# Batch-major copies of the mixer's B and C tiles on ScalarE, and factor loads in four transfers

## The chip, the cores and the metric

The kernel runs on one core of a Trainium2 chip. The metric is the device time of the whole program in microseconds (us). TensorE appears in the profile as PE (matrix products) and PEld (loads of its stationary operand), VectorE as DVE, ScalarE as ACT, GpSimd as POOL and SyncE, which issues nearly all DMAs here, as SP.

## The reference

The program is one decoder layer in fp32 for 4 sequences of 1024 tokens, 256 wide: a recurrent mixer, cross-attention and a mixture of experts. Only the mixer is touched. Cut to what matters, it computes for 32 heads with 32 states of 16 channels each:

```python
bc = einsum('bti,oi->bto', value, W_bc).reshape(B, T, 32, 4, 32)
bc = bc / (sqrt(sum(bc * bc, -1, keepdims=True)) + 1e-8)
Bz, Bx, Cz, Cx = bc[..., 0, :], bc[..., 1, :], bc[..., 2, :], bc[..., 3, :]
def step(z, s):                       # one token
    S = 1 / (1 + dt * k + dt * dt * A)
    z = S * (z - dt * A * s + dt * Bz * u)
    s = s + dt * z + dt * Bx * u
    y = sum_n(Cz * z) + sum_n(Cx * s)
```

## The kernel before

The mixer works through 16 units `u` of 64 time steps of all four batches, 256 columns, stored with time outside and batch inside: column `4t + b`. Each unit has four group pairs `gp`, of two head groups each; a head group is four heads, and a head has 32 partitions (a lane group). Within a unit the recurrence is turned into matrices: VectorE steps a 2x2 transition `phi` through 64 steps (`evolve`, L917 and L923), scales the four projections B and C by norms and by decay factors, and multiplies them with `phi` (`inputs` L956 to L970 for B, `read_out` L978 to L993 for C). The results are written back into `bc`.

TensorE then reads `bc` one batch at a time, so with a step of four numbers (16 bytes): it transposes the B tiles (`inputs_turned`, L629, `bc` as stationary operand), forms the causal products B times C (`causal_products`, L642, both operands from `bc`) and applies C to the carried state (`mixed_states`, L662, `bc` as moving operand), followed by L672 and L682. Between these stand the projections of the group pair that comes three places later (L604, 32 matmul records for each half) and the sums of squares for its norms (L618). Once in a unit there are the output products of the unit before (L691).

ScalarE evacuates projections (L757, L760), computes norms with three table loads (L767 to L771), scales the step coefficients of the next unit (`coefs`, L738, after their DMA) and copies transposes (L779). VectorE multiplies the norms by further factors (`factors`, L943); SyncE stores them to DRAM (L495) and loads them back, broadcast to the 32 partitions of each lane group, as `fb` and `fc` (L502).

Every engine works through its own list in the order in which the code writes it, and semaphores tie the lists together. So a wait on one instruction holds back all that is written behind it on that engine. The order of VectorE in a unit is, in short: `read_out` 0, `post` 3 of the unit before, `factors`, `ends`, `inputs` 1, `read_out` 1, `residual`, `inputs` 2, `mask` 0, `read_out` 2, `factors`, `post` 0, `inputs` 3, `mask` 1, `read_out` 3, then `evolve` of the next unit in pieces with `post` and `mask` between them, and `inputs` 0 of the next unit. `post` (L1013 to L1023) folds TensorE's result into output and state and uses `m1` and `m2`, the scratch tiles that `inputs` and `read_out` use too.

Of the kernel before, what the change touches and what calls it, by code (L numbers as in the profile page):

```python
# [13 lines left out]
P = 128  # L14
# [12 lines left out]
LANES = G * CH  # L27
EPS_LN, EPS_BC = 1e-5, 1e-8
# [14 lines left out]
def constants():  # L43
# [4 lines left out]
    hn = np.arange(G)[None] * J + jn[:, None]  # L48
    c["sel"] = (hn[:, :, None] == np.arange(H)[None, None]).astype(np.float32)
    c["causal"] = (np.arange(L)[None] >= (np.arange(P) % L)[:, None]).astype(np.float32)  # L50
    r = np.ones((P, UT), np.float32)
# [284 lines left out]
def mixer(nc, d, st, wbc, x, x1):  # L336

    with ExitStack() as ctx:
# [10 lines left out]
        sel = sb("sel", [P, G, H])  # L349
        causal = sb("causal", [P, L])  # L350
        resetm = sb("resetm", [P, UT])
# [10 lines left out]
        uu = sb("uu", [P, 2, 2, LANES])  # L362
        pinv = sb("pinv", [P, G, UT])
        iqe = sb("iqe", [P, LANES])
        pend = sb("pend", [P, 2, LANES])
# [11 lines left out]
        m1 = sb("m1", [P, 2, UT])  # L377
        m2 = sb("m2", [P, 2, UT])
# [45 lines left out]
        out_ready = sem("out_ready")  # L424
        bt_full = sem("bt_full")
# [13 lines left out]

        xv = x.rearrange("(q r u s) m -> u r s q m", q=2, r=2, s=L)  # L440
# [148 lines left out]
        def _(pe):  # L589
# [18 lines left out]
            def summed(u, gp, i):  # L608
# [7 lines left out]
                for v in range(2):  # L616
                    c = first + v
                    mm = pe.matmul(ssp[H * c:H * c + H, 0:UT], sel[:, g, :], sq[:, v, :],  # L618
                                   start=(i < 2), stop=(i >= 2))
                mm.then_inc(sums_done, 1)  # L620

            def inputs_turned(u, gp):
                n = GP * u + gp
                pe.wait_ge(in_ready, n + 1)
                if n > 0:
                    pe.wait_ge(km_ready, n)
                for v in range(2):
                    for b in range(B):
                        mm = pe.transpose(kp[:, v, b * P:(b + 1) * P],  # L629
                                          turns(bc[:, gp, v].rearrange("p i t -> p (i t)"))[:, :, b], ident[:])  # L630
# [17 lines left out]
            def mixed_states(u, gp, more, un, gn):  # L648
# [8 lines left out]
                for b in range(B):  # L657
                    for i in range(2):
                        for v in range(2):
                            for j in range(J):  # L660
                                r = slice(N * j, N * j + N)
                                pe.matmul(yp[r, b * L:(b + 1) * L], hpad[r, v, i, b, :],  # L662
                                          turns(bc[r, gp, 2 + v, i, :])[:, :, b],
# [60 lines left out]
        def _(act):  # L724
# [55 lines left out]

            def states(u, gp):
# [18 lines left out]
            for u in range(NU):  # L800
                for gp in range(GP):
                    un, gn = (u, GP - 1) if gp == 0 else (u + 1, gp - 1)
                    more = un < NU
                    inputs_turned(u, gp)
                    if more:
                        projected(un, gn, 0)
                        projected(un, gn, 1)
                    states(u, gp)
# [5 lines left out]
                    if more:  # L814
                        projected(un, gn, 2)
                        projected(un, gn, 3)
                        norms(un, gn)
                    if gp == 0 and u + 1 < NU:
                        coefs(u + 1)

        @block.vector
        def _(dve):
# [107 lines left out]
            def accumulate(u):  # L930
                for h in range(2):
                    dve.wait_ge(ln_ready, G * u + B * h + B)
                    v = pinv[:, B * h:B * h + B, :].rearrange("p g (t b) -> p (g t) b", b=B)
# [11 lines left out]
            def ends(u):  # L945
                dve.wait_ge(pinv_ready, u + 1)
                dve.wait_ge(iqe_in, 64 * (u + 1))
                link(V.tensor_copy(pend[:, 1, :].rearrange("p (g b) -> p g b", b=B), pinv[:, :, UT - B:UT]))
# [3 lines left out]
            def inputs(u, gp):  # L952
                n = GP * u + gp
                dve.wait_ge(fb_in, 128 * (n + 1))
# [1156 lines left out]
```

## Time and profile before

| | us |
|---|---|
| median of 3 runs | 3303.73 |
| lowest, highest | 3301.38, 3319.04 |
| profiled execution, whole time | 3292.49 |
| its span, first to last instruction | 3290.7 |
| busy in the span: PE, PEld, DVE, ACT, POOL | 2919.8, 2169.8, 2064.4, 1304.7, 286.7 |
| mean granted TensorE clock | 0.937 |

Busy time is the time in which an engine had an instruction at work. The mixer's units fill about 400 to 2090 us of the span; projections come before, cross-attention and experts behind. These rows of the page, in 40 slices of 82 us, show the mixer in slices 5 to 25:

```profile
PE   5885799999999999999999999589888399999996
DVE  5444898889889998999899888465562000111110
ACT  3443445454545554545454544133241021333332
PEclk9887899999999999999999999689899599999998
```

### The profile page before, as it was taken

Reading aid. Unit: us, or ns where it says so; the run is one execution under the profiler, and the core shown is the slowest. Engines: PE = TensorE matmul, PEld = TensorE weight load, DVE = VectorE, ACT = ScalarE, POOL = GpSimd, SP = SyncE. Lnnn points to the kernel's source line nnn. Section 1 sums busy time; section 2 is a strip of 40 time slices with the busy share of each in tenths; the row PEclk is TensorE's granted clock in tenths of the full one; section 3 lists DMA queues with packets and bytes.
Section 4 is the critical chain, followed back from the end, with each engine's and each line's share of the span. In section 5 each row is a group of like instructions: output and inputs, shape, how many; then the busy total and the mean of one; then the engine's idle time right before and its main releaser. Section 6 shows DMA issues by size and latency. Waiting matters only on the chain. (4 is left out here: it accounts for less than half of the span.)

```text
span 3290.7 us, 83944 instructions
## 1 busy us (share of the span) xinstructions
PE 2919.8 (89%) x34208; PEld 2169.8 (66%) x34208; DVE 2064.4 (63%) x7109; ACT 1304.7 (40%) x2250; POOL 286.7 (9%) x227
## 2 busy tenths in 40 slices
PE   5885799999999999999999999589888399999996
PEld 2343577777777877787788777433345166888885
DVE  5444898889889998999899888465562000111110
ACT  3443445454545554545454544133241021333332
POOL 0000000000000000000000000000004700443433
PEclk9887899999999999999999999689899599999998
DMA  6556333542444334433543352200053201778877
GB/s 235 151 151 177 91 85 77 121 104 76 95 117 104 81 95 118 108 83 88 124 104 87 82 128 69 79 1 1 1 203 113 98 28 36 208 201 204 207 200 216
DMA packets 333343, 373.98 MB, mean 114 GB/s; under 512 B 62395, under 2 KB 294988, under 8 KB 328268
## 3 DMA queue, kind: packets, MB, share of 16 engines
q1 hardware_dynamic: 310540, 340.22, 37.6%
q0 software_dynamic: 22464, 28.95, 4.3%
q8 instruction: 249, 4.08, 0.6%
q14 instruction: 90, 0.74, 0.1%
HBM read 269.18 MB, written 104.04 MB: 113 GB/s over the span
## 5 line engine op out<-in xcount | busy, mean ns | idle before, releaser
L604 PE MATMUL ring<-valt,wbc 128*128 128x256 f32 x4096 | 946.2, 387 | 29.0 <-DMA valt<-valt_scratch 26.9
L604 PEld LDWEIGHTS ring<-valt,wbc 128*128 128x128 f32 x4096 | 775.0, 193 | 169.4 <-issue 62.9
L757 ACT COPY bc<-ring 128x512 f32<-128x512 f32 x256 | 149.3, 583 | 739.1 <-PE ring L604 739.1
L917 DVE TENSOR_TENSOR uu<-phi,coef 128x64 f32<-128x64 f32 x2048 | 361.6, 218 | 2.1
L923 DVE TENSOR_TENSOR phi<-phi,uu 128x64 f32<-128x64 f32 x2048 | 361.3, 217 | 0.0
L2039 DVE TENSOR_SCALAR f_yr<-fp_y,f_meta 128x256 f32<-128x256 f32 x124 | 54.3, 480 | 413.3 <-PE fp_y L1856 413.3
L662 PE MATMUL yp<-bc,hpad 32*32 32x64 f32 x8192 | 260.2, 289 | 2.5 <-DVE hc L1023 2.5
L662 PEld LDWEIGHTS yp<-bc,hpad 32*32 32x32 f32 x8192 | 225.3, 121 | 53.3 <-issue 53.0
L1923 ACT ACTIVATE f_hT<-fp_h,f_b 128x256 f32<-128x256 f32 x248 | 117.4, 473 | 327.5 <-PE fp_h L1847 327.5
L1856 PE MATMUL fp_y<-f_w,f_hT 128*128 128x256 f32 x992 | 230.7, 386 | 7.9
L1723 POOL DMA_INDIRECT acc_scratch<-f_yr,f_meta x124 | 192.5, 1553 | 446.7 <-DVE f_yr L2039 300.1
L1847 PE MATMUL fp_h<-f_xrt,f_w 128*128 128x256 f32 x992 | 226.0, 381 | 0.8 <-ACT f_xrt L1912 0.8
L1710 POOL COPY f_xn<-f_gk 128x32 f32<-128x32 f32 x3 | 0.7, 242 | 2506.3 <-DVE f_rowid L2020 2502.9
L1856 PEld LDWEIGHTS fp_y<-f_w,f_hT 128*128 128x128 f32 x992 | 183.4, 190 | 45.0 <-ACT f_hT L1923 21.9
L1847 PEld LDWEIGHTS fp_h<-f_xrt,f_w 128*128 128x128 f32 x992 | 189.6, 191 | 27.3 <-issue 1.2
L618 PE MATMUL ssp<-sq,sel 128*32 128x256 f32 x1024 | 162.0, 394 | 41.0 <-ACT sq L760 40.7
L1972 DVE TENSOR_TENSOR xres<-fp_y,xres 128x1024 f32<-128x1024 f32 x10 | 12.2, 1225 | 268.9 <-PE fp_y L1778 134.8
L956 DVE TENSOR_TENSOR bc<-bc,fb 128x512 f32<-128x512 f32 x128 | 82.7, 687 | 129.0 <-DMA fb<-fac_scratch 128.4
L642 PEld LDWEIGHTS kp<-bc 32*64 32x64 f32 x8192 | 141.3, 203 | 32.2 <-issue 32.2
L1764 PE MATMUL fp_y<-f_ws,f_hT 128*128 128x256 f32 x512 | 124.6, 395 | 42.7 <-issue 42.7
L642 PE MATMUL kp<-bc 32*64 32x64 f32 x8192 | 153.0, 306 | 6.1 <-issue 3.7
L760 ACT ACTIVATE sq<-ring 128x512 f32<-128x512 f32 x256 | 153.1, 598 | 5.4 <-PE ssp L618 5.4
(227 smaller groups left out, 4070.9 us busy)
## 6 DMA issues: line engine op xcount, KB each, us to landing
f_w<-in_W_dram SPq DMA_DIRECT2D x128, 512.0 KB
coef<-par_scratch SPq DMA_DIRECT2D x128, 256.0 KB, 5.9
fb<-fac_scratch SPq DMA_DIRECT2D x512, 64.0 KB, 2.2
fc<-fac_scratch SPq DMA_DIRECT2D x512, 64.0 KB, 2.8
xg_scratch<-f_fill SPq DMA_DIRECT2D x16, 1032.0 KB, 17.3
f_xr<-xg_scratch SPq DMA_DIRECT2D x64, 258.0 KB
vtok_scratch<-p_vtok SPq DMA_DIRECT2D x32, 512.0 KB, 7.0
dub<-vtok_scratch SPq DMA_DIRECT2D x16, 1024.0 KB, 5.4
```

Source lines behind the costliest of these rows:

```text
L604: mm = pe.matmul(ring[:, p % 2, v * UT:(v + 1) * UT], wbc[:, k, g, first + v, :], valt[:, u % 2, k, :], start=(k == 0), stop=(k == 3))
L618: mm = pe.matmul(ssp[H * c:H * c + H, 0:UT], sel[:, g, :], sq[:, v, :], start=(i < 2), stop=(i >= 2))
L642: mm = pe.matmul(kp[L * i:L * i + L, j, b * L:(b + 1) * L], turns(bc[r, gp, v, i, :])[:, :, b], turns(bc[r, gp, 2 + v, i, :])[:, :, b], st ...
L662: pe.matmul(yp[r, b * L:(b + 1) * L], hpad[r, v, i, b, :], turns(bc[r, gp, 2 + v, i, :])[:, :, b], start=(b == 0 and i == 0 and v == 0), s ...
L757: nc.scalar.copy(bc[:, gp, first:first + 2, i // 2, :], o).then_inc(bc_ready, 1)
L760: nc.scalar.activation(sq[:], o, ACT.Square).then_inc(sq_ready, 1)
L917: made[k] = mark(V.tensor_tensor(uu[:, k].rearrange("p i (g b) -> p i g b", b=B), phi[:, t, ::-1, k, :].rearrange("p i (g b) -> p i g b", ...
L923: ins = V.tensor_tensor(phi[:, t + 1, :, k, :], phi[:, t, :, k, :], uu[:, k], ALU.add)
L1723: pool.indirect_dma_start(acc, bass.IndirectOffsetOnAxis(ap=meta[:, par, a, 0:1].bitcast(I32), axis=0), yr[:, par, a, :], None, compute_op ...
L1764: mm = pe.matmul(yp[:, 2 * (nb % 2) + a // 2, (a % 2) * DM:(a % 2 + 1) * DM], hT[:, e, f, a * P:(a + 1) * P], ws2[:, e, f, :], start=(e == ...
L1847: mm = pe.matmul(hp[:, f, 0:RT], w1[:, par, k, f * P:(f + 1) * P], xrt[:, par, k, :], start=(k == 0), stop=(k == 1))
L1856: mm = pe.matmul(yp[:, par, a * DM:(a + 1) * DM], hT[:, par, f, a * P:(a + 1) * P], w2[:, par, f, :], start=(f == 0), stop=(f == 3))
```

## The change

Four things change, all in the mixer.

1. `inputs` and `read_out` no longer write into `bc`. They write into new tiles `min_` and `mout`, in the same time-major order, and ScalarE copies these into `bc` in batch-major order (`turn_in`, `turn_out`: two copies of 128x512 each, four numbers of step on the reading side). TensorE's three readers of `bc` wait for the copies and read contiguous columns.
2. `min_` takes the place of `m1` and `m2` and also holds `uu` (scratch of `evolve`) and `pend` (scratch of `ends`). So `inputs`, `post`, `ends` and `evolve` on VectorE get waits on `turned_in`, and `read_out` one on `turned_out`.
3. Head rows in the factor and coefficient arrays in DRAM are ordered by lane group, then head group. A factor load is four DMAs of 128 KB in place of eight of 64 KB, and the coefficient and ratio loads read rows of 8 KB in place of 1 KB, with the same number of DMAs.
4. The call of `factors` behind `read_out` 2 moves inside it. `resetm` is halved, so the scans of `accumulate` are 16 of 128 elements in place of 8 of 256. `sel` is a sliding window of one narrow tile.

```diff
+        uu = min_[:, 1, 1, 0:4 * LANES].rearrange("p (k i l) -> p k i l", k=2, i=2)
+        pend = min_[:, 1, 1, 4 * LANES:6 * LANES].rearrange("p (i l) -> p i l", i=2)
...
-                return v.rearrange("(g j) t -> j g t", j=J)[j].unsqueeze(0).broadcast_to([N, G, v.shape[-1]])
+                return v.rearrange("(j g) t -> j g t", j=J)[j].unsqueeze(0).broadcast_to([N, G, v.shape[-1]])
...
-                src = st["fac"][n].rearrange("(c g i j) t -> g j i c t", c=4, g=GP, i=2)[gp]
+                src = st["fac"][n].rearrange("(c j g i) t -> g j c (i t)", c=4, j=J, g=GP)[gp]
                 for j in range(J):
-                    for c in range(2):
-                        sp.dma_start(dst[N * j:N * j + N, :, c, :],
-                                     src[j, :, c0 + c].unsqueeze(0).broadcast_to([N, 2, UT])).then_inc(signal, 16)
+                    sp.dma_start(dst[N * j:N * j + N].rearrange("p c i t -> p c (i t)"),
+                                 src[j, c0:c0 + 2].unsqueeze(0).broadcast_to([N, 2, 2 * UT])).then_inc(signal, 16)
...
             def inputs_turned(u, gp):
...
-                pe.wait_ge(in_ready, n + 1)
+                pe.wait_ge(turned_in, n + 1)
...
             def causal_products(u, gp):
...
-                pe.wait_ge(out_ready, n + 1)
+                pe.wait_ge(turned_out, n + 1)
...
-                                               turns(bc[r, gp, v, i, :])[:, :, b],
-                                               turns(bc[r, gp, 2 + v, i, :])[:, :, b],
+                                               by_batch(gp, v)[r, b * P + i * L:b * P + (i + 1) * L],
+                                               by_batch(gp, 2 + v)[r, b * P + i * L:b * P + (i + 1) * L],
...
+            def turn_batches(m, c, gp, done):
+                for v in range(2):
+                    ins = nc.scalar.copy(by_batch(gp, c + v).rearrange("p (b i t) -> p i b t", b=B, i=2),
+                                         m[:, v].rearrange("p i (t b) -> p i b t", b=B))
+                ins.then_inc(done, 1)
...
             def evolve(u, t0, t1):
...
                     if u > 0:
                         dve.wait_ge(out_ready, GP * u)
+                        dve.wait_ge(turned_in, GP * u)
...
             def accumulate(u):
-                for h in range(2):
+                for h in range(4):
...
             def inputs(u, gp):
...
-                    V.tensor_tensor(bc[:, gp, 0, i, :], fb[:, i, 1, :], m[:, 1, :], ALU.subtract)
-                    ins = V.tensor_tensor(bc[:, gp, 1, i, :], m[:, 0, :], fb[:, i, 0, :], ALU.subtract)
+                    V.tensor_tensor(min_[:, 0, i, :], fb[:, 1, i, :], min_[:, 0, i, :], ALU.subtract)
+                    ins = V.tensor_tensor(min_[:, 1, i, :], min_[:, 1, i, :], fb[:, 0, i, :], ALU.subtract)
                 ins.then_inc(in_ready, 1)
...
             def read_out(u, gp, between=None):
...
+                if between is not None:
+                    factors(between)
+                if n > 0:
+                    dve.wait_ge(turned_out, n)
...
             def post(u, gp, read):
...
-                dve.wait_ge(out_ready, read)
+                dve.wait_ge(turned_in, read)
```

On ScalarE, in the middle of a unit (from the last norm activation of group pair 0 on), the list reads before:

```order
L771 ACTIVATE nr<-nr 128x256
L738 ACTIVATE coef<-coef,nega 128x256 x8
L779 COPY btt<-kp 128x512 x2
L757 COPY bc<-ring 128x2x256
L760 ACTIVATE sq<-ring 128x512
L757 COPY bc<-ring 128x2x256
L760 ACTIVATE sq<-ring 128x512
L788 COPY hpad<-hc 128x2x4x16 x2
```

and now, with `mout` and `min` as the names of the new tiles:

```order
L776 ACTIVATE nr<-nr 128x256
L788 COPY bc<-mout 128x2x4x64 x2
L743 ACTIVATE coef<-coef,nega 128x256 x8
L784 COPY btt<-kp 128x512 x2
L762 COPY bc<-ring 128x2x256
L765 ACTIVATE sq<-ring 128x512
L788 COPY bc<-min 128x2x4x64 x2
L762 COPY bc<-ring 128x2x256
L765 ACTIVATE sq<-ring 128x512
L807 COPY hpad<-hc 128x2x4x16 x2
```

Two copies of the C tiles of group pair 1 stand ahead of the coefficients, and two of the B tiles of group pair 2 between the two evacuations behind them. A unit has eight such pairs: three stand ahead of these rows (the first, `turn_in` of group pair 0, is ahead of everything else of the unit), two behind them (the second of these, `turn_in` of group pair 3, is behind the next norms), and one in group pair 2.

On VectorE, at the end of `read_out` 2 and `post` 0, the list with its waits now reads as follows; before, L943 (now L981) stood behind the last row of `read_out`, and none of these rows waited for a copy.

```order
L1028 TENSOR_TENSOR fc<-phi,bc 128x2x256 [waits dve_step] x2
L981 TENSOR_TENSOR nr<-nr,pq 128x256 [waits nr_ready]
L1033 TENSOR_TENSOR mout<-phi,bc 128x2x256 [waits turned_out]
L1033 TENSOR_TENSOR mout<-phi,bc 128x2x256
L1037 TENSOR_TENSOR mout<-fc,mout 128x2x256 [waits dve_step] x2
L1057 SCALAR_TENSOR_TENSOR min<-valt,skip,yp 128x256 [waits sg_in,turned_in,y_full]
```

The factor multiply moved ahead of four instructions, and `post` 0 (L1057) now waits for `turned_in`, which is the pair of `min` copies shown in ScalarE's list.

On SyncE's queue, the DMAs from the loads of group pair 2 up to the coefficients were before:

```order
L502 DMA fb<-fac_scratch 32x2x256 x8
L482 DMA sg<-sg_scratch 128x1024
L502 DMA fc<-fac_scratch 32x2x256 x8
L470 DMA pq<-par_scratch 32x256 x3
L472 DMA iqe<-par_scratch 32x8x4 x4
L462 DMA coef<-par_scratch 32x8x256 x4
```

and are now:

```order
L507 DMA fb<-fac_scratch 32x2x512 x4
L488 DMA sg<-sg_scratch 128x1024
L507 DMA fc<-fac_scratch 32x2x512 x4
L476 DMA pq<-par_scratch 32x256 x3
L478 DMA iqe<-par_scratch 32x8x4 x4
L468 DMA coef<-par_scratch 32x2048 x4
```

Eight DMAs fewer are issued ahead of the coefficients, whose rows are now whole.

## Rows read from the trace of the kernel before

**Rows 1.** the mixer's stretch: busy us (instructions) of PE, PEld, DVE, ACT, POOL, PEclk

```profile
400.00:2090.00 1690.00, 1618.58 (x27937) 1311.88 (x27936) 1527.76 (x5744) 823.00 (x1358) 0.00 (x0) 0.98 0.39 96
```

**Rows 2.** timeline, the residual sum: start us, us, engine, line, names, shapes

```profile
492.45 0.68 DVE L1030 TENSOR_TENSOR xs<-yp,xs 128x512 f32<-128x512 f32 x1
...
2030.37 0.68 DVE L1030 TENSOR_TENSOR xs<-yp,xs 128x512 f32<-128x512 f32 x1
```

**Rows 3.** waits in 400 to 2090 us: us in total, times, longest us

```profile
DVE bc L956 <- DMA fb<-fac_scratch: 123.6, 30, 8.4
```

**Rows 4.** timeline, VectorE, one unit: in brackets idle us before and releaser

```profile
1245.02 0.41 DVE L970 TENSOR_TENSOR bc<-m,fb 128x256 f32<-128x256 f32 x1
...
1268.00 1.29 DVE L956 TENSOR_TENSOR bc<-bc,fb 128x512 f32<-128x512 f32 x2 [1.23 <-DMA fb<-fac_scratch]
...
1290.54 1.29 DVE L956 TENSOR_TENSOR bc<-bc,fb 128x512 f32<-128x512 f32 x2 [7.70 <-DMA fb<-fac_scratch]
...
1302.84 0.36 DVE L917 TENSOR_TENSOR uu<-phi,coef 128x64 f32<-128x64 f32 x2
...
1330.95 4.77 DVE L935 TENSOR_TENSOR_SCAN pinv<-resetm,pinv 128x256 f32<-128x256 f32 x8
...
1347.17 1.23 DVE L1001 TENSOR_TENSOR km<-kp,causal 128x1024 f32<-128x1024 f32 x1
...
1355.10 0.42 DVE L970 TENSOR_TENSOR bc<-m,fb 128x256 f32<-128x256 f32 x1
```

**Rows 5.** timeline, ScalarE, the same unit

```profile
1275.25 0.42 ACT L771 ACTIVATE nr<-nr 128x256 f32<-128x256 f32 x1
1284.31 3.30 ACT L738 ACTIVATE coef<-coef,nega 128x256 f32<-128x256 f32 x8 [8.65 <-DMA coef<-par_scratch]
...
1288.93 0.59 ACT L760 ACTIVATE sq<-ring 128x512 f32<-128x512 f32 x1
...
1307.21 0.42 ACT L771 ACTIVATE nr<-nr 128x256 f32<-128x256 f32 x1
```

**Rows 6.** timeline, TensorE, the same unit and an earlier one at half clock

```profile
1245.49 1.23 PE L629 MATMUL kp<-ident,bc 128*128 128x128 f32 x8
...
1258.99 2.38 PE L642 MATMUL kp<-bc 32*64 32x64 f32 x128
1261.29 3.72 PE L604 MATMUL ring<-valt,wbc 128*128 128x256 f32 x16
...
1289.58 1.07 PE L618 MATMUL ssp<-sq,sel 128*32 128x256 f32 x4 [5.38 <-ACT sq L760]
1290.58 2.39 PE L642 MATMUL kp<-bc 32*64 32x64 f32 x128
...
518.57 5.51 PE L604 MATMUL ring<-valt,wbc 128*128 128x256 f32 x16
```

**Rows 7.** timeline, the issuing queue of SyncE: start us, us of issuing, count

```profile
1266.81 4.25 SPq L502 DMA_DIRECT2D fc<-fac_scratch  x8
...
1275.57 2.08 SPq L462 DMA_DIRECT2D coef<-par_scratch  x4
```

**Rows 8.** DMA issues: count, KB each, median us from issue to landing

```profile
coef<-par_scratch SPq DMA_DIRECT2D x128, 256.0 KB, 5.9
dub<-vtok_scratch SPq DMA_DIRECT2D x16, 1024.0 KB, 5.4
```

**Rows 9.** groups by shape in 0 to 300 us: busy us, mean ns

```profile
L257 ACT COPY p_vraw<-pp_ring 128x512 f32<-128x512 f32 x32 | 18.7, 585 | 60.3 <-PE pp_ring L211 60.3
L253 ACT COPY p_xnt<-pp_ring 128x512 f32<-128x512 f32 x16 | 15.7, 1082 | 6.1 <-PE pp_ring L205 6.0
```

**Rows 10.** weight loads of 64 columns: duration ns min/median/max

```profile
L216 PEld LDWEIGHTS pp_ring<-p_xnt,p_win x32: 132/136/137, 42.3 to 237.7; 128*64 128x64 f32 x32
...
L691 PEld LDWEIGHTS yp<-wout,sg x512: 192/193/226, 480.5 to 2094.5; 128*64 128x64 f32 x171
```

**Rows 11.** window about a rest of TensorE, columns as in Rows 1

```profile
1286.80:1293.70 6.90, 4.12 (x134) 3.10 (x135) 3.16 (x6) 4.19 (x11) 0.00 (x0) 0.51 0.43 134
```

More of the change, by code:

```diff
@@ L27 @@
 LANES = G * CH
+SW = H + G - 1
 EPS_LN, EPS_BC = 1e-5, 1e-8
@@ L424, in mixer @@
         out_ready = sem("out_ready")
+        turned_in = sem("turned_in")
+        turned_out = sem("turned_out")
         bt_full = sem("bt_full")
@@ L779, in inputs_turned, with turn_in, turn_out @@
                     nc.scalar.copy(btt[:, v], kp[:, v, :].rearrange("p (b m) -> p b m", b=B)).then_inc(btt_ready, 1)
+            def turn_batches(m, c, gp, done):
[3 more added lines that the diff above has]
+                ins.then_inc(done, 1)
+            def turn_in(u, gp):
+                act.wait_ge(in_ready, GP * u + gp + 1)
+                turn_batches(min_, 0, gp, turned_in)
+            def turn_out(u, gp):
+                act.wait_ge(out_ready, GP * u + gp + 1)
+                turn_batches(mout, 2, gp, turned_out)
             def states(u, gp):
@@ L803, in _ @@
                     more = un < NU
+                    if gp == 0:
+                        turn_in(u, 0)
                     inputs_turned(u, gp)
@@ L806, in _ @@
                         projected(un, gn, 0)
+                    if gp == 1:
+                        turn_in(u, 2)
+                    if more:
                         projected(un, gn, 1)
+                    if gp == 0:
+                        turn_out(u, 0)
+                    if gp == 2:
+                        turn_out(u, 3)
                     states(u, gp)
@@ L815, in _ @@
                         projected(un, gn, 2)
+                    if gp == 0:
+                        turn_in(u, 1)
+                    if gp == 1:
+                        turn_out(u, 2)
+                    if more:
                         projected(un, gn, 3)
                         norms(un, gn)
-                    if gp == 0 and u + 1 < NU:
-                        coefs(u + 1)
+                    if gp == 0:
+                        turn_out(u, 1)
+                        if u + 1 < NU:
+                            coefs(u + 1)
+                    if gp == 1:
+                        turn_in(u, 3)
         @block.vector
@@ L947, in ends @@
                 dve.wait_ge(iqe_in, 64 * (u + 1))
+                dve.wait_ge(turned_in, GP * u + 1)
                 link(V.tensor_copy(pend[:, 1, :].rearrange("p (g b) -> p g b", b=B), pinv[:, :, UT - B:UT]))
@@ L963, in inputs, with read_out @@
                     need(scaled[i])
[L964 to L967 removed]
+                    V.tensor_tensor(split(fb[:, :, i]), rows(1, 0, 2 * gp + i), twice(bc[:, gp, 0, i, :]), ALU.mult)
+                if n > 0:
+                    dve.wait_ge(turned_in, n)
+                other = [mark(V.tensor_tensor(split(min_[:, ::-1, i]), rows(0, 1, 2 * gp + i), twice(bc[:, gp, 1, i, :]),
+                                              ALU.mult)) for i in range(2)]
+                for i in range(2):
                     need(other[i])
[L969 to L970 removed]
+                    V.tensor_tensor(min_[:, 0, i, :], fb[:, 1, i, :], min_[:, 0, i, :], ALU.subtract)
+                    ins = V.tensor_tensor(min_[:, 1, i, :], min_[:, 1, i, :], fb[:, 0, i, :], ALU.subtract)
                 ins.then_inc(in_ready, 1)
[L973 removed]
+            def read_out(u, gp, between=None):
                 n = GP * u + gp
[L975 removed]
+                dve.wait_ge(fc_in, 64 * (n + 1))
                 if gp == 0:
                     dve.wait_ge(pinv_ready, u + 1)
[L978 removed]
+                decayed = [mark(V.tensor_tensor(fc[:, :, i], fc[:, :, i],
                                                 pinv[:, 2 * gp + i, :].unsqueeze(1).broadcast_to([P, 2, UT]), ALU.mult))
@@ L1053, in _ @@
                 mask(u, 0)
-                read_out(u, 2)
-                factors(n0 + 3)
+                read_out(u, 2, n0 + 3)
                 post(u, 0, n0 + 3)
@@ L2072, in layouts @@
     r["A_states"] = np.asarray(inputs["L0_attn_A_log"]).reshape(G, J * N).T
-    r["dt_bias_b"] = np.tile(np.asarray(inputs["L0_attn_dt_bias"]), B)[:, None]
+    r["dt_bias_b"] = np.tile(np.asarray(inputs["L0_attn_dt_bias"])[rows], B)[:, None]
     r["ctxT"] = np.asarray(inputs["ctx_768"]).transpose(0, 2, 1)
```

61 lines of the change are left out of this document (27 added, 34 removed).

## The prediction

> **What bounds the kernel now.** I read the windows view of the mixer first. In its 1690 us TensorE is busy 1618.6, VectorE 1527.8 and ScalarE 823.0 [rows 1]. Two engines are over 90% busy, so busy shares don't say which one sets the time. The page's chain that ended last covers only the experts and is no help here; the period of a unit is. The residual sum comes once a unit, and from 492.45 to 2030.37 there are 14 periods of 109.85 us [rows 2].
>
> The timeline of one unit tells who sets that period. I count from the end of VectorE's `inputs` 0, 1245.43 (1245.02 plus 0.41) [rows 4]. VectorE works without a hole except for 1.23 us ahead of `inputs` 2 and 7.70 us ahead of `inputs` 3, both for the factor DMA [rows 4]; in the whole stretch that wait is 123.6 us in 30 places [rows 3]. It starts `evolve` at 1302.84, 57.4 us in, and ends the next `inputs` 0 at 1355.52, 52.6 us later (I take 52.6, start to start) [rows 4]. TensorE starts its transposes 0.06 us after `inputs` 0 [rows 6] and rests once, 5.38 us, for a square of ScalarE [rows 6], which in turn had stood 8.65 us in front of `coefs` for its DMA [rows 5]. So VectorE's own list sets the period: about 101 us of work and 8.9 us of waiting for factors. TensorE follows closely but isn't waited for.
>
> **What the change removes.** TensorE: the causal products take 2.30 us for 128 records (1258.99 to 1261.29) at full clock, and 2.32 us at half clock (1290.58 plus 2.39, less overlap) [rows 6, 11]. An array that is not sped up by its clock is limited by the reading of its operands. A 64-column weight load takes 136 ns from contiguous columns and 193 ns with a step of 16 bytes [rows 10]. By that ratio the products lose 0.7 us, by a halved rate 1.15; I take 1.0 each, with 0 and 1.15 as ends. `mixed_states` should gain more, but most of it stands behind the last sum of squares of a group pair, and nobody waits for it: it counts as nothing.
>
> DMA: a factor load of eight takes 4.25 us to issue [rows 7], so four take 2.1. The load `fc` 2 stands ahead of the coefficients on the queue, which are issued at 1275.57 and land for ScalarE at 1284.31, 8.7 us later [rows 5, 7]. Four issues fewer are 2.1 us; and `fc` 2, which started behind the issue of `fb` 2, can start at once when `read_out` 1 is done, 0.7 us earlier. So the coefficients start at about 1272.8. A megabyte in 8 KB rows (`dub`) lands in 5.4 us, while one quarter of that in 1 KB rows takes 5.9 [rows 8]. So the coefficients land at about 1278.2, 32.8 us into the unit. The factor load of group pair 3 is stored 2.4 us earlier by the moved multiply and is shorter: both DMA waits of VectorE go, 8.9 us.
>
> **What it adds.** Eight pairs of copies on ScalarE per unit, 128x512 each. The trace has no ACT instruction that reads SBUF with a step of 16 bytes. A copy that steps on its writing side takes 1082 ns, a contiguous one 585 [rows 9]. These are the ends: 1.2 or 2.1 us for a pair. I take 2.1, since TensorE's weight loads show that the stepped read itself is slower [rows 10].
>
> The Trainium skill has a rule for either end. In "SBUF — State Buffer", section "Door 1: The DMA port swizzle", it says that SBUF has 16-byte cachelines and an access that goes to a new line each time pays; by it a pair takes the long time. TensorE's stepped loads agree with it [rows 10]. In "ScalarE: Activation LUTs", section "Rules for kernel authors", a budget of about 0.3 us plus 0.83 ns per element knows no step; by it a pair takes 1.45 us, near the short case. The 1082 ns of a stepped write contradict this second rule [rows 9]; no row here shows the read.
>
> What these copies delay is the point. `post` 0 and `evolve` now wait for `turned_in`, and ScalarE's list is in lockstep with TensorE's. The new path from `inputs` 0 to `evolve`:
> - `turn_in` 0: 2.1.
> - TensorE's transposes to the end of the norms, 1245.49 to 1275.67: 30.2, less 1.0: 29.2 [rows 5, 6].
> - `turn_out` 1: 2.1. It ends 33.4 in, behind the landing of the coefficients, so that wait is gone.
> - `coefs`, transposes copied, first evacuation: 1284.31 to 1289.52, 5.2 [rows 5].
> - TensorE's sums (1289.58) to the end of the next norms (1307.63): 18.05, less 1.0 for the products and 0.8 for work that was done here at half clock (an estimate: half of the 1.07 of the sums, and the start of the projection behind): 16.2 [rows 5, 6].
> - `turn_in` 3: 2.1.
>
> That is 56.9 us (54.2 with short copies). `evolve` follows, and VectorE's remaining 52.6 us, plus 0.4 for scans: eight take 4.77 us [rows 4], so 16 half as long take somewhat more for their fixed part (0 to 1). The period is 109.9 us (107.2), against 109.85. The 8.9 us of DMA wait have become waits for ScalarE at `post` 0 and at `evolve`. The multiply that moved gains nothing more, because `post` 0 waits anyway. SyncE's shorter list is waited for by nobody else.
>
> **The clock.** TensorE now runs out of work. At the end of a unit it has finished everything but the values when VectorE makes the last mask, and then waits for `evolve`'s rest, `inputs` 0 (mask done at 1348.40, `inputs` 0 at 1355.52: 7.1 us [rows 4]) and `turn_in` 0: a rest of 7 to 9 us in each unit where it had none. The trace shows what follows a rest: after 5.38 us of it the granted clock is 0.51 in the window 1286.80 to 1293.70, with the work back at 1289.58 [rows 6, 11], so 4.1 us are worked at the 1.2 GHz level and 2.1 us lost; in another unit a 16-record projection took 5.51 us in place of 3.72 [rows 6]. Now that lost time stands at the head of the path. I take 2.1 per unit; ends 0 and 3.4 (the whole window at half clock). Before, such rests were rare, with a mean clock of 0.98, and lay in VectorE's shadow [rows 1].
>
> **Sum.** Period 109.9 + 2.1 = 112.0, 2.15 more than before; 15 repeats give +32. The prologue waits for its first coefficients too; half of such a wait saved is -4 (estimate from the 8.65). The last unit's chain gets one more pair of copies, +2. Total +30. The profiled execution's own time is 3292.5 (span 3290.7), so it would be 3322; the median of the runs is 11.2 us above that execution, and on its footing the forecast is 3334 us.
>
> **Rivals.**
> 1. Short copies and the clock loss: 109.3 a unit, -8 in all, with the ends -2: 3294. For it: the copy that took 1082 ns steps on its writing side, and reading may be another matter [rows 9].
> 2. Long copies, no clock loss (TensorE's rest is broken up by small work): +1 -2, 3303.
> 3. The other side: ScalarE copies at the contiguous 585 ns and the clock holds. Then VectorE is the bound again except for some 6 us at `post` 0 and `evolve`; 107.2 a unit, -40 -2: 3262. It decides below about 0.9 us a copy when the clock holds, or below 0.5 us when it doesn't. Against it: the slow stepped loads and the half clock after a rest [rows 10, 11].
> 4. The change doesn't do what it says: contiguous columns don't speed the products, because it is the many small instructions that limit them. Then 2.0 more per unit: 3364. Against it: the stepped loads again, 193 ns for 136 [rows 10]. Of like size: coefficients that still take 8.7 us from their issue would land at 36.1, 2.7 later than ScalarE needs them, +40: 3374; a landing between the two is likelier.
>
> **Chances.** Forecast 0.46; rival 1 0.21; rival 2 0.15; rival 3 0.12; rival 4 0.06. A measurement here tells a change of 0.5%, 16.5 us, from none: faster is below 3287, slower above 3320. Rival 3 and a third of rival 1 are faster: with some spread 0.22. Rival 2 and the rest of rival 1, and a tenth of the forecast for a smaller clock loss, are the same: 0.29. Slower 0.49. The range takes rival 3 at its lower end and rival 4 at its upper: 3264 to 3360. The forecast's own range is 3315 to 3354 (clock loss 0.8 to 3.4).
>
> **What the profile after would show.** Right: no DMA wait on VectorE's L956 successor; idle there ahead of `post` 0 (some 5 us or more) and ahead of `evolve`; copies of 1.08 us; causal products near 1.3 us; TensorE busy at least 64 us less in the mixer (64 products, 1.0 each), with a rest of over 7 us at each unit's end and a clock near 0.93 there against 0.98 [rows 1]; coefficients landed before ScalarE asks. Wrong: copies near 0.6 us; a wait ahead of `inputs` 3 that is still the factor DMA's; a mixer clock unchanged; VectorE's period near 101.

## The result, and the profile after

The changed kernel takes 3410.18 us (median of 4 runs, 3408.04 to 3413.32) where the kernel before, on the same chip, takes 3311.39 (4 runs, 3301.38 to 3324.01). The ratio is 1.0311, with a 95% interval from 1.026 to 1.0362. So it is slower, as forecast, but by 99 us and not by 30, and the time lies above the range.

These rows of the windows view cover 14 units of the mixer each, from the second residual sum to the sixteenth; first the kernel before. The columns are those of [rows 1].

```profile
492.45:2030.37 1537.92, 1484.76 (x25069) 1202.17 (x25068) 1404.78 (x5322) 764.90 (x1259) 0.00 (x0) 0.98 0.40 98
```

The kernel after:

```profile
497.09:2146.60 1649.51, 1406.39 (x25092) 1117.16 (x25091) 1413.32 (x5434) 996.52 (x1484) 0.00 (x0) 0.92 0.37 91
```

A unit takes 1649.51 / 14 = 117.8 us where it took 109.85 [rows 2] and 112.0 were forecast. TensorE is busy 5.6 us less in each unit (1484.76 less 1406.39, over 14), ScalarE 16.5 more, and the clock fell from 0.98 to 0.92. What the engines wait for is seen in the waits view of the kernel after, 400 to 2090 us, first VectorE, then TensorE (us in total, times, longest us):

```profile
DVE min L1057 <- issue: 88.8, 15, 8.2
DVE min L955 <- ACT bc L788: 73.0, 15, 7.1
DVE min L1006 <- ACT bc L788: 41.6, 14, 3.5
DVE mout L1033 <- ACT bc L788: 26.6, 18, 1.7
DVE bc L995 <- DMA fb<-fac_scratch: 4.1, 7, 1.3
```

```profile
PE kp L634 <- ACT bc L788: 113.4, 14, 8.6
PE yp L677 <- issue: 39.9, 22, 4.0
PE yp L687 <- issue: 30.1, 13, 4.1
PE yp L687 <- DVE km L1045: 28.8, 18, 4.0
PE kp L647 <- issue: 13.7, 4, 3.7
PE kp L634 <- issue: 4.1, 3, 2.6
```

VectorE's wait for factor rows has gone from 123.6 [rows 3] to 4.1. In its place it stands 230 us for ScalarE's copies (L788); the row that names "issue" ahead of `post` (L1057) is the wait for `turned_in` too: in the unit below it starts at 1351.53, and the copies of `turn_in` 2 end at 1351.44. TensorE stands 8 us a unit for the first copy, and loses 88 us to "issue": it waits for nothing but its own instructions. In the same stretch of the kernel before, those "issue" rows come to 22.5 us. The row `L687 <- DVE km` is another thing: there TensorE really waits for VectorE's mask (`mask`, L1045), and goes on 0.04 us behind it.

The timeline of one unit shows where each piece lies. ScalarE (in brackets the idle us before, and the releaser):

```profile
1340.21 0.42 ACT L776 ACTIVATE nr<-nr 128x256 f32<-128x256 f32 x1
1340.53 2.10 ACT L788 COPY bc<-mout 128x512 f32<-128x512 f32 x2
1342.53 3.30 ACT L743 ACTIVATE coef<-coef,nega 128x256 f32<-128x256 f32 x8
1345.74 1.04 ACT L784 COPY btt<-kp 128x512 f32<-128x512 f32 x2
1348.34 0.58 ACT L762 COPY bc<-ring 128x512 f32<-128x512 f32 x1 [1.55 <-PE ring L609]
...
1367.72 0.42 ACT L776 ACTIVATE nr<-nr 128x256 f32<-128x256 f32 x1
1368.04 2.11 ACT L788 COPY bc<-min 128x512 f32<-128x512 f32 x2
```

TensorE in the same unit:

```profile
1308.55 1.97 PE L634 MATMUL kp<-ident,bc 128*128 128x128 f32 x8 [8.63 <-ACT bc L788]
...
1341.78 0.85 PE L687 MATMUL yp<-km,dub 128*32 128x64 f32 x19 [3.35 <-issue]
1342.56 1.97 PE L634 MATMUL kp<-ident,bc 128*128 128x128 f32 x8
1344.32 7.43 PE L609 MATMUL ring<-valt,wbc 128*128 128x256 f32 x32
1351.68 0.63 PE L623 MATMUL ssp<-sq,sel 128*32 128x256 f32 x4
...
1375.06 1.59 PE L647 MATMUL kp<-bc 32*64 32x64 f32 x128
```

VectorE:

```profile
1351.53 0.48 DVE L1057 SCALAR_TENSOR_TENSOR min<-valt,skip,yp 128x256 f32<-128x256 f32 x1 [6.36 <-issue]
...
1370.29 0.36 DVE L955 TENSOR_TENSOR min<-phi,coef 128x64 f32<-128x64 f32 x2 [4.13 <-ACT bc L788]
```

The hole (a gap in TensorE's work) of 3.35 us ahead of 1341.78 belongs to TensorE's supply of instructions. The DMA view of the kernel after, from 1334.0 to 1339.3 us, has only the data queue in it, at 93% of 16 engines:

```profile
q1 hardware_dynamic: 427, 1.15, 93.4%
```

and from 1339.3 to 1341.9, while TensorE stands, one packet of the queue that brings instructions, with the data queue nearly idle:

```profile
q1 hardware_dynamic: 37, 0.03, 3.1%
q8 instruction: 1, 0.02, 2.5%
```

That packet holds 16 KB, starts at 1339.33 and takes 1.04 us; TensorE goes on 1.4 us after its end. One such packet comes for each 256 instructions of TensorE, products and weight loads. This row is the kernel before's 14 units, in which TensorE ran 50137 instructions:

```profile
q8 instruction: 196, 3.21, 1.0%
```

This is no chance at one place. In the 14 units of the changed kernel TensorE has 43 gaps of over 0.3 us that the waits view puts down to "issue", 88 us together, and each of them ends 1.2 to 1.8 us after the end of a packet of this queue; in the traces of all other kernels here it is 1.0 to 1.8 us, without exception.

In the kernel before, the packet of the place shown starts in the middle of the second part of `mixed_states` (at 1272.76), and the hole is 0.46 us (ahead of 1275.61). Counted from the same instruction, it starts 2.6 us later in the changed kernel.

### The profile page after: what moved, and what is told of

It reads as the page before. It is cut to its first block and busy times, and to the rows that moved or that the text cites. A ratio compares the mean times of both kernels' runs of the same rounds, so it can differ in the third digit from the quotient of the medians.

```text
span 3406.3 us, 83816 instructions
## 1 busy us (share of the span) xinstructions
PE 2823.0 (83%) x34208; PEld 2068.5 (61%) x34208; DVE 2073.7 (61%) x7237; ACT 1568.7 (46%) x2506; POOL 286.7 (8%) x227
## 5 line engine op out<-in xcount | busy, mean ns | idle before, releaser
L609 PE MATMUL ring<-valt,wbc 128*128 128x256 f32 x4096 | 987.3, 399 | 29.0 <-DMA valt<-valt_scratch 26.2
L609 PEld LDWEIGHTS ring<-valt,wbc 128*128 128x128 f32 x4096 | 805.5, 201 | 177.3 <-issue 61.1
L955 DVE TENSOR_TENSOR min<-phi,coef 128x64 f32<-128x64 f32 x2048 | 359.2, 215 | 73.5 <-ACT bc L788 73.0
L961 DVE TENSOR_TENSOR phi<-phi,min 128x64 f32<-128x64 f32 x2048 | 358.8, 215 | 0.0
L634 PE MATMUL kp<-ident,bc 128*128 128x128 f32 x512 | 96.1, 348 | 148.7 <-ACT bc L788 144.6
L788 ACT COPY bc<-min 128x512 f32<-128x512 f32 x128 | 136.8, 1122 | 107.6 <-DVE min L1011 107.6
L623 PE MATMUL ssp<-sq,sel 128*32 128x256 f32 x1024 | 160.6, 392 | 22.5 <-ACT sq L765 13.9
L634 PEld LDWEIGHTS kp<-ident,bc 128*128 128x128 f32 x512 | 75.7, 178 | 158.5 <-ACT bc L788 147.9
L667 PEld LDWEIGHTS yp<-bc,hpad 32*32 32x32 f32 x8192 | 123.8, 107 | 56.9 <-issue 54.1
L667 PE MATMUL yp<-bc,hpad 32*32 32x64 f32 x8192 | 144.5, 220 | 5.8 <-DVE hc L1067 2.8
```

What stands on the lines that cost most here:

```text
L609: mm = pe.matmul(ring[:, p % 2, v * UT:(v + 1) * UT], wbc[:, k, g, first + v, :], valt[:, u % 2, k, :], start=(k == 0), stop=(k == 3))
L623: mm = pe.matmul(ssp[H * c:H * c + H, 0:UT], sel[:, G - 1 - g:G - 1 - g + H], sq[:, v, :], start=(i < 2), stop=(i >= 2))
L634: mm = pe.transpose(kp[:, v, b * P:(b + 1) * P], by_batch(gp, v)[:, b * P:(b + 1) * P], ident[:])
L667: pe.matmul(yp[r, b * L:(b + 1) * L], hpad[r, v, i, b, :], by_batch(gp, 2 + v)[r, b * P + i * L:b * P + (i + 1) * L], start=(b == 0 and i ...
L955: made[k] = mark(V.tensor_tensor(uu[:, k].rearrange("p i (g b) -> p i g b", b=B), phi[:, t, ::-1, k, :].rearrange("p i (g b) -> p i g b", ...
L961: ins = V.tensor_tensor(phi[:, t + 1, :, k, :], phi[:, t, :, k, :], uu[:, k], ALU.add)
```

## The experiments

Sixteen kernels ran. "Instructions" are TensorE's gaps of over 0.3 us that are put down to "issue", "mask" its gaps of over 0.3 us for VectorE's mask, both summed over 14 units; "unit" is the mean of 14 units of the profiled execution.

| | ratio to before | 95% interval | unit, us | instructions, us | mask, us |
|---|---|---|---|---|---|
| before | 1 | | 109.85 | 21 | 2 |
| after | 1.0311 | 1.026 to 1.0362 | 117.82 | 88 | 29 |
| e1, DMA part alone | 0.9952 | 0.9925 to 0.998 | 109.65 | 40 | 0 |
| e16, e1 again | 0.9958 | 0.9936 to 0.998 | 109.68 | 40 | 0 |
| e7, e1 and coefficients early | 0.9975 | 0.9951 to 0.9999 | 109.95 | 26 | 13 |
| e3, flat copies | 1.0236 | 1.0182 to 1.029 | 114.63 | 94 | 18 |
| e6, coefficients early | 1.0253 | 1.018 to 1.0326 | 115.75 | 77 | 28 |
| e13, stepped products | 1.0318 | 1.0272 to 1.0364 | 117.27 | 30 | 0 |
| e5, rest filled with 32 | 1.0432 | 1.0367 to 1.0497 | 119.46 | 77 | 25 |
| e5b, filled with 16 | 1.0224 | 1.0161 to 1.0288 | 115.85 | 98 | 21 |
| e4, turn 3 first | 1.0109 | 1.0048 to 1.0169 | 113.14 | 89 | 0 |
| e8, turn 2 first | 1.0326 | 1.0261 to 1.0392 | 117.96 | 96 | 17 |
| e10, both turns | 1.008 | 1.0051 to 1.0108 | 112.62 | 91 | 0 |
| e9, e10 and coefficients early | 1.0046 | 1.0013 to 1.0079 | 112.02 | 75 | 2 |
| e11, e10 filled with 16 | 1.0044 | 1.0018 to 1.0071 | 111.62 | 83 | 0 |
| e12, e10 and direct transposes | 0.9971 | 0.994 to 1.0002 | 109.75 | 78 | 3 |
| e15, e12 and coefficients early | 0.9999 | 0.9973 to 1.0024 | 110.34 | 79 | 11 |
| e14, e12 filled with 6 | 0.9958 | 0.9932 to 0.9985 | 108.73 | 75 | 3 |

By the ratio alone e3, e5b and e6 can't be told from the changed kernel, since the intervals overlap. Their unit is the finer measure, though it is one execution each: e1 and e16, the same kernel on two chips, have 109.65 and 109.68.

**The DMA part alone (e1, e16, e7).** e1 is the kernel before with the row order, the four transfers, the narrow `sel` and, in `read_out` 2, the earlier multiply of the factors:

```
-dve.wait_ge(fb_in, 128 * (n + 1))
+dve.wait_ge(fb_in, 64 * (n + 1))
...
-read_out(u, 2)
-factors(n0 + 3)
+read_out(u, 2, n0 + 3)
```

> The kernel before, with the change's layout of the factors in DRAM (rows ordered by lane group), its four transfers of 2 KB rows, its selection matrix and its earlier product of the factor rows; no copies on ScalarE, products of before. Theory A: the two waits for factor rows on the path of a unit (8.9 us together) go, and nothing else is longer; the next to be late is TensorE, busy 95 us of a unit, so a unit takes 101 to 104 us instead of 109.85 and the kernel 3180 to 3240 us. Rival: what is loaded earlier makes the coefficients late in turn, and the time stays at 3290 to 3310 us. Either way all of the loss of the changed kernel (+99 us), and more, belongs to the copies.

Measured: 0.9952, a unit 0.2 us shorter. Theory A failed. The time (3284.06) lies below the rival's 3290 to 3310 too, and the reason is another. The wait for factor rows halves, but VectorE waits for ScalarE's norms instead, and TensorE is full. Waits, 400 to 2090 us, and the window of its 14 units:

```profile
DVE bc L955 <- DMA fb<-fac_scratch: 60.9, 29, 3.9
DVE nr L942 <- ACT nr L770: 34.4, 15, 4.6
```

```profile
490.10:2025.26 1535.16, 1494.51 (x25166) 1211.65 (x25153) 1407.40 (x5321) 768.57 (x1260) 0.00 (x0) 0.99 0.40 98
```

TensorE is busy 1494.5 us of 1535.2 here, and its gaps for instructions are 39.7: next to nothing is left for waiting on others. In the kernel before, the two came to 1484.8 and 21.3 of 1537.9, so its waits for other engines were 2.3 us a unit at most, and with its gaps as they were, no more than that could be won by taking waits away; the 8.9 us of waiting on VectorE were mostly slack. The whole loss of the changed kernel belongs to the copies, the products that read them and what hangs on both.

> The kernel of e1 again, beside e15 on the same chip, to tell which of the two is the better version. Theory: 0.993 to 0.998 of before, TensorE being busy 96% of the mixer in both; if e15 is at 0.994 the two can't be told apart.

> As e1, and the second half of the coefficients is asked for right behind the first. Theory A (its transfer stands in the way of TensorE's instructions near the end of group 0): 3 us a unit less than e1, 40 us in all. Rival: it makes no difference (within 10 us of e1), since in the kernel before the hole at that place was 0.46 us only.

e16 repeats e1's ratio. In e7 the second `load_coefs(u + 1, i)` is moved right behind the first: no gain (0.9975), as the rival had it, and the factor rows are waited for as before (120.2 us).

**How long the copies are (e3).**

```
-nc.scalar.copy(by_batch(gp, c + v)... "p (b i t) -> p i b t", m[:, v]... "p i (t b) -> p i b t")
+nc.scalar.copy(by_batch(gp, c + v), m[:, v].rearrange("p i t -> p (i t)"))
```

> The changed kernel with copies that read in order of addresses; it leaves out the reordering by batch. Each copy should take 0.58 us instead of 1.12, a pair 1.1 instead of 2.1. Theory A: three pairs lie on the path that sets the period (turn of inputs 0, of outputs 1, of inputs 3), so a unit is 3.0 us shorter, the kernel 45 us (3365), and up to 80 us if the sums of squares come earlier as well. Rival: the period is set by TensorE and the holes in it, and the time moves by less than 10 us.

The copies by their line's view, first the changed kernel, then e3 (duration ns min/median/max):

```profile
L788 ACT COPY bc<-min x128: 1072/1119/1166, 364.0 to 2175.3; 128x512 f32<-128x512 f32 x128
```

```profile
L788 ACT COPY bc<-min x128: 601/614/630, 365.0 to 2126.5; 128x512 f32<-128x512 f32 x128
```

A pair is 1.0 us shorter and a unit 3.2 us: three pairs lie on the path, as Theory A had it. The step costs 0.5 us a copy.

**Where the copies stand in ScalarE's list (e4, e8, e10, e9).** e4 and e8 are one move each, e10 is both:

```
+turn_in(u, 3)            # e4: gp 1, ahead of norms(u + 1, 0)
 norms(un, gn)
-turn_in(u, 3)
```

```
 turn_out(u, 1)           # e8: gp 0
+turn_in(u, 2)            # was in gp 1, behind projected(un, gn, 0)
 coefs(u + 1)
```

> The changed kernel; in group 1 ScalarE turns the scaled inputs of group 3 ahead of the three functions of the norms instead of behind them (its source is ready 4 us before the norms begin, and VectorE stands 4.13 us for it before it can begin the next unit's evolution). Theory A: the 4.1 us lie on the path that sets the period, since the norms have slack (their next reader comes 15 us later): a unit is 3.5 to 4.1 us shorter, the kernel 1.012 to 1.016 of before. Rival: TensorE (rests and holes) sets the period, and evolution begins earlier only to wait elsewhere: 1.026 or more.

> The changed kernel; ScalarE turns the scaled inputs of group 2 right behind the outputs of group 1, ahead of the scaling of the coefficients, not behind the next two slots' work: VectorE stands 6.4 us for it before the state update of group 0. Theory A: the update and what follows come 4 to 6 us earlier, but evolution still waits for the turn behind the norms, which hangs on TensorE's sums: under 1 us a unit, 1.027 to 1.032 of before. Rival B: everything behind the update is on the path: 4 us a unit, 1.015.

> The changed kernel with both turns moved (groups 2 and 3) and the second half of the coefficients asked for early. Theory A: VectorE's waits for these copies (6.4, 4.1 us) and part of the hole go together, 8 to 10 us a unit, and TensorE (101 us busy and some 6 us of holes) is the next bound: a unit 108 to 110 us, the kernel 0.99 to 1.005 of before. Rival: 1.01 or more, the copies' rest in TensorE at the start of each unit (8.6 us) keeping it from less.

> The changed kernel with both turns (groups 2 and 3) moved ahead of the norms and of the coefficients; the coefficients asked for as in the changed kernel, so that factor rows do not wait behind them (in e9 VectorE waited 108 us for these). Theory A: a unit 109 to 111 us, the kernel 0.99 to 1.003 of before. Rival B: like e9 (1.0046) or like e4 (1.011), the larger hole in TensorE taking back what the factor rows give.

e4 takes 4.7 us off a unit, somewhat more than the 3.5 to 4.1 of Theory A. VectorE's wait for L788 at `evolve` falls from 73.0 to 7.1 us, 4.4 for each of its 15 times, and since VectorE comes earlier, TensorE no longer waits for the mask (29 us before):

```profile
DVE min L956 <- ACT bc L788: 7.1, 4, 1.8
```

e8 alone gives nothing: that wait grows from 73.0 to 105.6 instead.

```profile
DVE min L954 <- ACT bc L788: 105.6, 15, 7.1
```

Theory A held for both in its reason. e10 gave less than its Theory A (112.6, not 109 to 111) and came out as Rival B, between e9 and e4; e9, with the coefficients early, can't be told apart from it: VectorE's wait for factor rows is 108.1 us in e9. Its unit of 112.0 misses its 108 to 110 too. So VectorE's list was not the only path left; what TensorE's rest at the unit's head costs is tested next.

**TensorE's rest and its clock (e5, e5b, e11, e14).** Products that nobody reads are put behind the last `mixed_values` of a unit:

```
+for _ in range(FILL):   # 32 in e5, 16 in e5b and e11, 6 in e14
+    pe.matmul(kp[:, 2, 0:UT], ident[:], wout[:, 0, :], start=True, stop=True)
```

> The changed kernel with 32 further products (7.1 us by the same kind's duration) in TensorE's rest of 8.6 us at each unit's start, written to a bank that nobody reads. Theory A (the rest costs TensorE's clock: behind it 8 transposes take 1.97 us for 1.09 and 32 projection products 9.06 us for 7.07): these go back to full speed, a unit is 2 to 3 us shorter, the kernel 1.018 to 1.024 of before. Rival: the clock comes back but what waits next is VectorE or ScalarE, and the time stays at 1.029 or more.

> The changed kernel with 16 further products ahead of the rest at each unit's start. In e5 each of the 32 ran as two, 14.1 us a unit where 7.1 were meant, and the unit's transposes came 5.4 us late; 16 take 7.0 us and fit into the rest of 8.6. Theory A: full clock behind the rest (32 projection products 7.07 us instead of 9.06), 1 to 3 us a unit off, the kernel 1.018 to 1.026 of before. Rival: what the slow clock costs TensorE is hidden by VectorE and ScalarE there, no gain: 1.028 or more.

e5 was mis-sized: one such product runs as two records of 0.22 us, so 32 took 14.08 us and made the next transposes late, 1.2% slower than the changed kernel. e5b is the test. TensorE's 8 transposes and 32 projection records at a unit's head are back at full clock (in e5 1.04 and 7.07 us, from 1.97 and 9.06). From the first transpose to the sums they take 10.55 us in the changed kernel and 7.92 in e5b, means of 14 units, and in e5b a unit is 2.0 us shorter: Theory A. The wait at the head is nearly gone:

```profile
PE kp L635 <- ACT bc L793: 10.8, 9, 1.6
```

> e10 with the 16 further products of e5b. Theory A: 1 to 3 us a unit less than e10, 0.975 to 0.995 of before, TensorE being the bound once both copies are out of VectorE's way. Rival: equal to e10 within its interval.

> e12 with 6 further products (2.6 us) ahead of the rest at the unit's start, which in e12 is 3.6 us by the mean. Theory A: part of the clock comes back, 0.2 to 0.4% less than e12 (0.993 to 0.995 of before). Rival: nothing or a loss (0.997 to 1.0), since in e12 the hole of up to 4 us at the end of group 0 lowers the clock just as well.

Both gain 1.0 us a unit on the kernel they start from (e10, e12). For e11 this is the low end of the 1 to 3 us, and its ratio of 1.0044 is far from 0.975 to 0.995; e14 gains 0.13% where 0.2 to 0.4 were expected. The intervals overlap, so each alone is not certain.

**Whether TensorE has to wait for the first copy (e12, e15).** The transposes of group 0 read `min_` in steps, as before the change:

```
-pe.wait_ge(turned_in, n + 1)
+pe.wait_ge(turned_in if gp else in_ready, n + 1)
-src = by_batch(gp, v)[:, b * P:(b + 1) * P]
+src = ... if gp else turns(min_[:, v])[:, :, b]
+dve.wait_ge(bt_full, 2 * GP * u + 2)       # before min_ is reused
```

> e10, but TensorE's transposes of group 0 read the scaled inputs before they are turned (in steps, as before the change) and so do not wait for ScalarE's copies; VectorE waits for them before it reuses that tile. Theory A: TensorE's rest at the unit's start is 2.1 us shorter (the transposes themselves 0.14 us longer), a unit 1.5 to 2.1 us less than e10: 0.007 of before less. Rival: the rest's end is not what sets TensorE's pace there, and it equals e10.

> e12 with the second half of the coefficients asked for early, a version that may beat both kernels. e9 against e10 says 0.3% less: 0.993 to 0.995 of before. Rival: the factor rows wait for the coefficients and it stays at 0.997.

A unit is 2.9 us shorter than e10's, 1.5 to 2.1 were expected. TensorE's rest there is 8.1 us in the changed kernel, 5.2 in e10 and 3.6 in e12, and the clock of the 14 units 0.92, 0.94 and 0.96; from the first transpose to the sums it takes 10.0 us in e10 and 9.6 in e12. This is TensorE's row in e12's waits:

```profile
PE kp L636 <- DVE min L1013: 46.9, 13, 5.6
```

Asking for the coefficients early (e15) did not help: 0.9999, an interval that overlaps e12's, and a unit 0.6 us longer. The factor rows are waited for 113.6 us, as its rival had it.

**What makes TensorE stand for instructions (e6, e13).**

> The changed kernel; the second half of the coefficients is asked for right behind the first, 11 us earlier. The hole of 3.35 us in TensorE's products at the end of group 0 began with its block of instructions coming 2.6 us after the products had passed the same place at which it came in the kernel before. Theory A (the block stands behind the 8 KB packets of the coefficients): the hole shrinks to 0.5 to 1.5 us, a unit is 2 to 3 us shorter, the kernel 30 to 45 us (3365 to 3380). Rival B (TensorE runs through 256 short products faster than blocks come, whatever else is moved): hole 2.5 us or more, time within 10 us of 3410.

> The changed kernel, but TensorE's causal products and its products with the states read the turned tiles in steps of four, as the kernel before read its own (they take the wrong columns: this leaves the right pairing of batches out). So they take 2.38 us and 1.11 + 2.96 us again, 2.7 us a group more than in the changed kernel. Theory A (holes come where TensorE runs through a block of its instructions faster than the next one comes): the holes of the mixer, 116 us in 14 units, fall to 25 to 60 us, though nothing in the transfers is changed; of the 10.6 us a unit that the products cost, 4 to 6 come back, and the kernel is at 1.035 to 1.05 of before. Rival B (the larger transfers delay the blocks): the holes stay at 90 us or more, and the kernel is at 1.06 or more.

e6 moves the transfer that stood in front of the instruction packet. The packet now starts 0.5 us later in TensorE's course than in the kernel before, not 2.6. The hole at that place shrinks to the upper end of what was expected, in this unit to 1.51 us, and the transposes behind it run at full clock:

```profile
1336.22 0.53 PE L687 MATMUL yp<-km,dub 128*32 128x64 f32 x19 [1.51 <-issue]
1336.68 1.09 PE L634 MATMUL kp<-ident,bc 128*128 128x128 f32 x8
```

A unit is 2.1 us shorter. But all gaps for instructions together only fall from 88 to 77 us: others open elsewhere. e13 leaves every transfer alone and lets the causal products and those with the states read in steps again. They then take the wrong columns, so e13 leaves out the right pairing of batches:

```
-by_batch(gp, v)[r, b * P + i * L:b * P + (i + 1) * L]
+turns(bc[r, gp, v, i, :])[:, :, b]        # and so for the C tiles
```

Its TensorE waits (400 to 2090 us) and its 14 units:

```profile
PE kp L634 <- ACT bc L788: 106.0, 14, 8.1
PE yp L687 <- issue: 11.5, 7, 2.9
PE yp L677 <- issue: 11.4, 7, 2.7
PE kp L647 <- issue: 5.0, 3, 2.5
```

```profile
499.41:2141.24 1641.83, 1505.05 (x25090) 1218.47 (x25089) 1413.92 (x5434) 998.59 (x1484) 0.00 (x0) 0.96 0.37 92
```

TensorE's gaps for instructions fall from 88 to 30 us, 4.2 a unit, and its waits for the mask from 29 to nothing, 2.0 a unit. The products' rows are 10.7 us a unit longer (2.38, 1.11 and 2.96 us for 1.59, 0.65 and 1.54, four times), of which a higher clock elsewhere (0.96 for 0.92) gives back a part: TensorE is busy 7.0 us a unit more (1505.05 less 1406.39, over 14). The unit is 117.3 us, no longer than the changed kernel's, and the ratio of 1.0318 lies below the 1.035 to 1.05 of Theory A. So Theory A holds in its reason: it is chiefly the speed of the products that makes TensorE outrun its instructions. And more comes back than it had: in this kernel the gaps, the waits for the mask and the clock together take back all that the faster products give.

Transfers have a part at single places. At the one shown the packet of e13 is 1.6 us later than in the kernel before, with a hole of 1.63 us, and that of e6 only 0.5 us, so there the coefficients' transfer counts for more than the speed. What decides when a packet is asked for was not measured.

## Why the prediction was right or wrong

- **Copies of 2.1 us a pair: right** (2 x 1.12; ends were 1.2 and 2.1). With 1119 ns stepped and 614 ns flat, the copies depend on the step. The cacheline rule of the Trainium skill ("SBUF — State Buffer", "Door 1: The DMA port swizzle") agrees. The per-element budget of the Trainium skill ("ScalarE: Activation LUTs", "Rules for kernel authors") fits neither copy: its 0.73 us, an estimate from that page, is too long for the flat one and too short for the stepped.
- **Products: right in size.** The causal products take 1.59 us for 2.38, so 0.8 less where I took 1.0.
- **Factor waits gone, coefficients in time: right** [rows 3, 5]: 4.1 us are left, and `coefs` follows `turn_out` 1 without a wait.
- **The path through ScalarE: right.** From `inputs` 0 (1306.3) to `evolve` (1370.29) it is 64.0 us, forecast 59.0 with the clock; VectorE's rest of the unit is 53.0, as forecast. That the copies lie on it is what e4 shows clear of noise, and e3's unit bears it out.
- **The clock after the rest: right in kind, a little small.** 2.1 were forecast; the work at the unit's head is 2.6 us longer than in e5b, and e5b's unit 2.0 shorter.
- **Wrong: the step from `coefs` to TensorE's sums, "5.2".** It took 9.15 us (1342.53 to 1351.68). The forecast had it end with ScalarE's square; it ended with TensorE's projection. With a hole of 0.46 us and the clock at full, TensorE would have reached its sums at 1347.3, just ahead of the 1347.7 that 5.2 us give. It came 4.4 us later: 2.9 are the hole (3.35 for 0.46) and 1.5 the half clock behind it, in the last products (0.3), the transposes (0.8) and the start of the projection (0.4). I had read [rows 5, 6] as if TensorE were ahead there, since it rested 5.38 us for a square. But that rest was ScalarE's 8.65 us of waiting for coefficients, passed on, and the change takes just this wait away: what was left of the lead was some 0.4 us. And I gave no thought to what feeds TensorE when its instructions get shorter. Of the 1.1 us of the path that remain, 0.8 lie ahead of the norms, nearly all of it the clock, and 0.3 behind the sums.
- **Wrong: `mixed_states` "counts as nothing".** It halved (96 records in 1.54 us for 2.96), and of the changed kernel's 88 us of gaps for instructions 68 lie in the short products right behind it (L677, L687). e13 slows it together with the causal products, so the share of each is not shown; but its gain wasn't nothing, it was turned into a hole.
- **Wrong, though the forecast did not rest on it alone: "VectorE's own list sets the period. TensorE isn't waited for".** e1 takes half the DMA waits away and gains 0.2 us a unit. TensorE was the bound, and VectorE's waits were slack behind it. In the changed kernel this did not matter, since the new path is longer than both.
- **The signs** that were to show the forecast right nearly all came, with the time outside the range: idle ahead of `post` 0 and `evolve`, a rest of 8.1 us, a clock of 0.92. None of them looks at TensorE's gaps for instructions. Rival 4 came nearest to the reason, "the many small instructions", but as a limit on each product's time, and the products did get faster.
- **Two sums don't come out.** The range of 3264 to 3360 leaves out the rivals' own 3262, 3364 and 3374, and the parts named for "the same" add up to 0.34, not 0.29. Neither touches the miss.

The size: 5.8 us a unit over the forecast, of which the unit above shows 5.0 on its path (it is 0.8 us shorter than the mean). Over 15 units that is 87 us, and the profiled execution is 86 us over its forecast (3408 for 3322). The miss of the median is 76, nearly all of the difference because the 11.2 us that were added between the two measured 2.1.

## What to carry to other kernels

Where one engine is busy over 95% and another waits often, first take the waits away in a test: if the time stays, they are slack. Before an engine's rest is counted as room, ask what it rests for, and whether the change takes that wait away. A copy handed to a "free" engine stands in that engine's list, and what it waits for there decides its price: here moving one pair of copies ahead of three table loads was worth 4.7 us of 117.8, and letting TensorE read the unturned tile once was worth 2.9. Before making hundreds of short instructions faster, look for "issue" ahead of them: where the instruction stream can't follow, as here, faster ones gave nothing. Whether fewer would help was not tried.

The best versions are e1 (with e16) and e14, both some 0.4 to 0.5% faster than the kernel before; they can't be told apart. e14 keeps the whole change, with two pairs of copies moved, direct transposes and six idle products.

## What the runs showed of the hardware

- TensorE's instructions come in packets of 16 KB, one per 256 instructions, on a DMA queue of their own that shares the 16 engines with data. In the changed kernel 353 instructions ahead of the hole shown took 2.8 us (1335.43 to 1338.20), so 256 of them some 2 us, an estimate from these rows; TensorE stood up to 4.1 us at such places (longest of L687's waits). Every gap of over 0.3 us for instructions ended 1.0 to 1.8 us behind the end of a packet, in the 14 units of all 18 traces.
- What a hole does to the clock differs. Behind the one of 3.35 us the transposes ran at the 1.2 GHz level (1.97 us, granted clock 0.50), behind that of 1.51 us in e6 at 2.4 GHz (1.09 us, 1.00). In e10 they took 1.11 us behind a hole of 3.25 us (0.99), and the clock fell only in the projection that followed, 8.76 us for 7.07 (0.80). The windows, in this order, the last two for e10:

```profile
1341.70:1344.40 2.70, 2.62 (x28) 2.45 (x29) 1.74 (x3) 2.70 (x6) 0.00 (x0) 0.50 0.27 88
1336.20:1337.60 1.40, 1.38 (x27) 1.29 (x28) 1.14 (x3) 1.39 (x3) 0.00 (x0) 1.00 0.04 12
1303.00:1304.50 1.50, 1.43 (x28) 1.34 (x29) 0.42 (x1) 1.50 (x3) 0.00 (x0) 0.99 0.29 98
1304.50:1313.10 8.60, 8.60 (x34) 7.03 (x32) 7.84 (x16) 6.74 (x14) 0.00 (x0) 0.80 0.66 152
```

- A stepped read by ScalarE costs about as much as the stepped write of [rows 9]: 1119 ns against 1082.
